# Another order of the steps, and 58 dummy matmuls at 12 of the maxima's and exponentials' steps

## The chip, the cores and the metric

The kernel runs on one core of a Trainium2 chip. The metric is the device time of one execution in microseconds (us), as the median of several runs. Five engines work side by side, each on its own list of instructions in program order: TensorE (PE, matmuls; its weight loads are shown apart as PEld), VectorE (DVE), ScalarE (ACT), GpSimd (POOL) and SyncE (SP, which issues most transfers). They wait for each other through semaphores alone.

## The reference, cut to what matters

The input x is 4 batches of 512 tokens of 128 features. The result is x plus two branches of its layer norm xn:

```
x  = L0_attn_x                       # (4, 512, 128)
xn = layernorm(x)
attn = Wo( chunk_attention(xn, chunk=16) + chunk_attention(every third token of xn, chunk=16) )
h  = xn + mla(rmsnorm(xn))           # 16 heads, causal attention over 512 tokens, latent q and k/v, rope
ffn = h + moe(rmsnorm(h))            # a shared expert and 7 routed ones, 2 picked for each token
out = x + attn + ffn
```

Everything is in float32. In `mla` the causal scores need the maximum of each row before the exponential, so the scores are computed twice: once with queries in the rows for the maxima, once transposed with the maxima already subtracted.

## The kernel before, in words

The work is cut into 760 steps. A table, ORDER (L152 on), names them in one sequence, and every engine walks through that same sequence and issues its own part of each step it has one in. So the table sets the order of work on every engine, and the semaphores alone set when it happens. A step is written as kind and numbers, the first number being the batch 0 to 3:

- LN, STATS, ROOT, XT, MA, MB, MV, WF: layer norm statistics, transposes of the normalised tokens, and the projections of the causal attention. ST are the transfers of the split bf16 parts of q and k into two stacks, SHIFT turns the maxima of one group of four heads into rows of the q stack.
- S (maxima): scores of one unit into a bank of ring A (two PSUM banks); VectorE reduces them to `neg_max` (L1012).
- E (exponentials): the same scores transposed into a bank of ring B (three banks), which ScalarE reads through the exponential into `p_mla` (L830). PV multiplies those with v into `bank_c`, Y, YT, X1 carry the result on.
- LQ, LK, LV, KD, VD, LS, LR, PT, LO, LT, LW: the two chunked attentions. LS also writes into ring A.
- R2, R3, X2T, ROUTE, PICK: second norm and routing. GU and DOWN: the eight experts, 32 steps of each; GU uses ring B, DOWN ring A.

A `*` in the table stands for the next maxima step and, once there is one, the next exponentials' step; `*3` for three of them. There are 176 maxima and 176 exponentials' steps, and the exponentials run 22 steps behind the maxima. Where an S stands directly ahead of an E, TensorE issues the two together, matmul by matmul (L1180 for E, L1159 for S, then the masks, L1166): one works on 64 rows of the array, the other on the other 64. TensorE waits for both banks (`wait_free`) before such a pair.

WARM (L64) is a table of dummy matmuls ahead of certain steps: float32, `eye` times `eye`, 128 columns, into `bank_c` (L1192). There are 30 of them.

Of the kernel before, what the change touches and what calls it, by code (L numbers as in the profile page):

```python
# [167 lines left out]
LR.2.2 *2 PT.2.2 PICK.0.0 LT.2.1 * LS.2.3 LO.2.2 PICK.0.1 LR.2.3 ST.3.2 * PICK.0.2 PV.2.0.1 PT.2.3 * LT.2.2 *
PV.2.0.2 PV.2.0.3 LS.2.4 MV.3 *3 KD.3.0 SHIFT.2.2 *3 PICK.0.3 * Y.2.0 R2.1 * ST.3.3 PV.2.1.0 KD.3.1 * KD.3.2 LO.2.3
KD.3.3 R3.1 ST.3.4 ST.3.5 LR.2.4 PV.2.1.1 * PV.2.1.2 PT.2.4 *3 X2T.1 * SHIFT.2.3 PV.2.1.3 * ST.3.6 * LT.2.3 *2 Y.2.1  # L170
PV.2.2.0 * LO.2.4 VD.3.0 * LS.3.0 LR.3.0 ROUTE.1 PV.2.2.1 PV.2.2.2 LT.2.4 *2 LW.2 PT.3.0 * PV.2.2.3 ST.3.7 SHIFT.3.0
* LS.3.1 * Y.2.2 PV.2.3.0 *2 LO.3.0 LR.3.1 * PT.3.1 *3 LT.3.0 LS.3.2 LO.3.1 PV.2.3.1 * PV.2.3.2 PV.2.3.3 VD.3.1
LR.3.2 *2 SHIFT.3.1 Y.2.3 PT.3.2 LT.3.1 PICK.1.0 PICK.1.1 LS.3.3 YT.2 LO.3.2 PICK.1.2 *2 LR.3.3 PICK.1.3 X1.2
PV.3.0.0 PT.3.3 *5 LT.3.2 * PV.3.0.1 * SHIFT.3.2 LS.3.4 PV.3.0.2 * PV.3.0.3 *3 Y.3.0 *2 WX LO.3.3 LR.3.4 * PV.3.1.0
* PT.3.4 * LT.3.3 PV.3.1.1 LO.3.4 * PV.3.1.2 PV.3.1.3 SHIFT.3.3 LT.3.4 *3 Y.3.1 * LW.3 R2.2 *3 PV.3.2.0 *4 PV.3.2.1
PV.3.2.2 *2 PV.3.2.3 *2 Y.3.2 *4 R3.2 PV.3.3.0 * PV.3.3.1 *2 GU.0.0 GU.0.1 PV.3.3.2 PV.3.3.3 DOWN.0.0 Y.3.3 GU.0.2
DOWN.0.1 GU.0.3 DOWN.0.2 GU.0.4 YT.3 DOWN.0.3 GU.0.5 DOWN.0.4 GU.0.6 DOWN.0.5 X1.3 GU.0.7 DOWN.0.6 R2.3 GU.1.0
DOWN.0.7 GU.1.1 R3.3 X2T.2 DOWN.1.0 GU.1.2 DOWN.1.1 GU.1.3 ROUTE.2 PICK.2.0 X2T.3 DOWN.1.2 GU.1.4 DOWN.1.3 PICK.2.1
GU.1.5 DOWN.1.4 GU.1.6 DOWN.1.5 PICK.2.2 GU.1.7 DOWN.1.6 PICK.2.3 ROUTE.3 GU.2.0 DOWN.1.7 GU.2.1 PICK.3.0 DOWN.2.0
GU.2.2 DOWN.2.1 GU.2.3 DOWN.2.2 GU.2.4 PICK.3.1 DOWN.2.3 GU.2.5 DOWN.2.4 GU.2.6 PICK.3.2 DOWN.2.5 GU.2.7 DOWN.2.6  # L180
GU.3.0 PICK.3.3 DOWN.2.7 GU.3.1 DOWN.3.0 GU.3.2 DOWN.3.1 GU.3.3 DOWN.3.2 GU.3.4 DOWN.3.3 GU.3.5 DOWN.3.4 GU.3.6
DOWN.3.5 GU.3.7 DOWN.3.6 DOWN.3.7
# [1232 lines left out]
```

How the kernel before makes its waits and increments, by code:

```python
        def wait_full(eng, use):  # L452
            ring, i, n = where[use]
            eng.wait_ge(full[ring][i], n)
# [1 line left out]
        def wait_drained(eng, use):  # L457
            ring, i, n = where[use]
            eng.wait_ge(drained[ring][i], n)
# [1 line left out]
        def wait_free(eng, use):  # L462
            ring, i, n = where[use]
            if n > 1:
                eng.wait_ge(drained[ring][i], n - 1)
# [21 lines left out]
        @block.sync  # L488
# [26 lines left out]
                kind, b = step[0], step[1] if len(step) > 1 else 0  # L515
                if kind == "LV" and step[2] == (QUADS - 1) // 4:
                    for n in range(step[2] + 1):
                        wait_drained(sp, ("LV", b, n))
                    for top in range(2):
                        n, at = P - CHUNK * (1 - top), P + CHUNK * (2 * top - 1)
                        sp.dma_start(v_dram[b, top, 0:n], v_rows[0:n, 0:X // 2]).then_inc(v_out, 16)
                        sp.dma_start(v_dram[b, top, at:at + P], v_rows[:, X // 2:]).then_inc(v_out, 16)
                if kind == "VD":
                    i0, i1 = SEGMENTS[step[2]]
                    sp.wait_ge(v_out, V_OUT * (b + 1))
                    if step[2]:
                        wait_full(sp, ("LO", b, LOCAL_UNITS - 1))
                    elif b:
                        wait_full(sp, ("LO", b - 1, NLU - 1))
                    else:
                        sp.wait_ge(v_zeroed, 1)
                    for top in range(2):
                        of = v_dram[b, top, CHUNK * top:CHUNK * top + 2 * P, :, i0:i1, :].rearrange(
```

## Time and profile before

| | us |
|---|---|
| median of 3 runs | 375.98 |
| lowest and highest | 373.47, 378.34 |
| the profiled execution | 371.83 |
| its span, first to last instruction | 369.6 |

In that execution TensorE is busy 90% of the span, VectorE 77%, ScalarE 60%, GpSimd 33%. The first maxima step stands at 26 us, the first exponentials' step at 60 us, the first expert at 273 us. In the rows further down a busy time is in us unless it says ns, "x8" counts instructions, "idle before" is how long the engine had nothing running just ahead, and the name behind the arrow is what released it.

### The profile page before, as it was taken

The numbers are of one execution on the slowest core, as the hardware profiler recorded it, in microseconds if no ns is written. First come the engines' busy times: TensorE is split into PE (matmuls) and PEld (weight loads), VectorE is DVE, ScalarE is ACT, GpSimd is POOL, SyncE is SP. The second block draws the span as 40 slices with busy tenths as digits, with TensorE's granted clock in tenths as the row PEclk, the third lists the DMA queues.
The fourth block names the chain that finished last, engine by engine and source line by source line (L and its number), as shares of the span: only waits on it lengthen the run. The fifth ranks groups of instructions, "written<-read, shape, count | busy, mean of one in ns | idle before, by whom it ended". The sixth has DMA issues, their size and how long they took to land.

```text
span 369.6 us, 11664 instructions
## 1 busy us (share of the span) xinstructions
PE 334.2 (90%) x4504; PEld 206.3 (56%) x4504; DVE 285.0 (77%) x720; ACT 222.3 (60%) x545; POOL 123.0 (33%) x148
## 2 busy tenths in 40 slices
...
PEclk9999999999999989999998999989999999999998
...
GB/s 200 77 108 173 71 167 62 67 62 42 40 162 46 36 66 51 78 184 25 43 53 50 65 65 34 36 3 172 5 0 0 3 27 2 4 28 2 29 0 28
DMA packets 29141, 21.84 MB, mean 59 GB/s; under 512 B 12312, under 2 KB 26008, under 8 KB 29048
## 3 DMA queue, kind: packets, MB, share of 16 engines
...
q10 hardware_dynamic: 216, 0.20, 0.2%
...
## 4 chain that ended last, share of the span: by engine, by line
PE 60%; DVE 28%; issue 5%; ACT 3%; DMA 3%; SPq 1%; POOL 0%; DVEq 0%; ACTq 0%; POOLq 0%
PE bank_B L1372 13%; DVE neg_max L1012 9%; PE bank_B L1180 8%; PE bank_c L1276 7%; PE bank_A L1378 7%; PE bank_A L1318 3%; PE bank_M L1283 2%; PE bank_B L1166 2%; DVE s_loc L1029 2%; DVE row_max L1026 2%; PE bank_M L1341 2%; PE bank_M L1221 2%; PE bank_c L1192 2%; PE bank_M L1211 1%; PE bank_M L1326 1%
## 5 line engine op out<-in xcount | busy, mean ns | idle before, releaser
L830 ACT ACTIVATE p_mla<-bank_B 128x512 f32<-128x512 f32 (+1 forms) x176 | 92.0, 561 | 54.6 <-PE bank_B L1166 31.0
L1012 DVE TENSOR_REDUCE neg_max<-bank_A 128x1 f32<-128x512 f32 (+3 forms) x176 | 106.9, 636 | 15.8 <-PE bank_A L1166 13.0
L1180 PE MATMUL bank_B<-q_stack,k_stack 54*128 54x512 bf16 (+3 forms) x256 | 62.4, 306 | 12.1 <-DVE neg_max L1012 8.2
L1159 PE MATMUL bank_A<-k_stack,q_stack 52*128 52x512 bf16 (+3 forms) x256 | 63.1, 307 | 3.2 <-DMA q_stack<-parts 2.2
L1372 PE MATMUL bank_B<-xrT,k_diag 128*128 128x512 f32 x128 | 60.9, 597 | 1.1 <-DVE k_diag L1137 1.1
L703 POOL TENSOR_TENSOR x<-x,q_part 128x512 f32<-128x512 f32 x31 | 39.5, 1274 | 58.0 <-ACT q_part L864 41.7
L1276 PE MATMUL bank_c<-p_mla,v_mla 128*32 128x384 f32 (+12 forms) x512 | 47.6, 453 | 0.4 <-ACT p_mla L830 0.4
L1180 PEld LDWEIGHTS bank_B<-q_stack,k_stack 54*128 54x128 bf16 x256 | 19.4, 94 | 49.6 <-issue 23.4
L864 ACT ACTIVATE q_part<-bank_A,expert_w 128x128 f32<-128x128 f32 x108 | 30.8, 369 | 24.6 <-PE bank_A L1378 24.6
L1137 DVE SCALAR_TENSOR_TENSOR k_diag<-k_diag,bank_B 128x512 f32<-128x512 f32 x32 | 22.0, 687 | 29.1 <-ACT k_diag L848 26.7
L1166 PE MATMUL bank_A<-masks 64*128 64x64 bf16 (+2 forms) x352 | 43.9, 204 | 0.0
L1166 PE MATMUL bank_B<-masks 64*128 64x64 bf16 (+2 forms) x352 | 43.8, 204 | 0.0
L1378 PEld LDWEIGHTS bank_A<-k_diag 128*128 128x128 f32 x256 | 33.1, 191 | 14.1 <-issue 14.1
L1166 PEld LDWEIGHTS bank_B<-masks 64*128 64x128 bf16 x352 | 32.6, 97 | 12.8 <-issue 0.9
L609 POOL TENSOR_TENSOR nrm<-nrm,half 128x8 f32<-128x8 f32 (+1 forms) x8 | 10.7, 1332 | 73.4 <-DVE nrm L1088 65.1
L1378 PE MATMUL bank_A<-k_diag 128*128 128x128 f32 x256 | 33.9, 275 | 0.7 <-DVEq L1145 0.7
L1166 PEld LDWEIGHTS bank_A<-masks 64*128 64x128 bf16 x352 | 32.8, 97 | 1.8
L1372 PEld LDWEIGHTS bank_B<-xrT,k_diag 128*128 128x128 f32 x128 | 21.6, 191 | 18.0 <-issue 13.6
L1142 DVE TENSOR_TENSOR k_diag<-bank_B,k_diag 128x512 f32<-128x512 f32 x32 | 22.1, 691 | 1.1
L1159 PEld LDWEIGHTS bank_A<-k_stack,q_stack 52*128 52x128 bf16 x256 | 19.3, 94 | 6.3 <-issue 3.7
L848 ACT ACTIVATE k_diag<-bank_B 128x512 f32<-128x512 f32 x32 | 19.5, 610 | 3.6 <-PE bank_B L1372 3.6
L1318 PE MATMUL bank_A<-k_diag,q_part 128*32 128x128 f32 x544 | 20.1, 277 | 0.7 <-DVE neg_max L1012 0.7
...
## 6 DMA issues: line engine op xcount, KB each, us to landing
...
```

The source lines that it names most:

```text
L703: link(nc.gpsimd.tensor_tensor(x[:, tb, :], x[:, tb, :], weighted[down_no[step] % 2], ALU.add))
L830: drained_by(nc.scalar.activation(p_of(n)[:, m:m + len(heads), 0:w], src, ACT.Exp, scale=SCALE), step)
L864: ins = nc.scalar.activation(weighted[n % 2][:, i, :], down[:, i, :], ACT.Copy, scale=expert_w[:, c * NT + i, e - 1:e])
L1012: drained_by(nc.vector.tensor_reduce(neg_max[:, g, m:m + len(heads), i], src, AX.X, ALU.max, negate=True), step)
L1142: ins = nc.vector.tensor_tensor(hid[n % 2], bank_of(step + (1,))[:], hid[n % 2], ALU.mult)
L1159: return nc.tensor.matmul(bank_of(step)[:, n * w:(n + 1) * w], q_stack[b % 2][rows, h % 8, i * P:(i + 1) * P], k_stack[b % 2][rows, h % 8, ...
L1166: return nc.tensor.matmul(to, half_eye[half, low, :], triangle[half, :].unsqueeze(1).broadcast_to((SLOT, len(heads), SLOT)), start=False, ...
L1180: nc.tensor.matmul(bank_of(step)[:, m * w:(m + 1) * w], k_stack[b % 2][rows, h % 8, j * P:(j + 1) * P], q_stack[b % 2][rows, h % 8, j * P: ...
L1276: last = nc.tensor.matmul(bank_c[32 * m:32 * m + width, j * P:], heads[:, first:first + width], p_of(n)[:, m, 0:S - j * P], start=(j == 0) ...
L1318: last = nc.tensor.matmul(bank[PAIR * j:PAIR * j + PAIR, c:c + P], q_part[:, a, pair, :], k_diag[:, a, :, CHUNK * pair:CHUNK * pair + CHUN ...
L1372: full_by(nc.tensor.matmul(bank_of(use)[:], w_exp[:, e, m, :], x2T[:, c, :], start=True, stop=True), use)
L1378: last = nc.tensor.matmul(bank[:, i * D:(i + 1) * D], hid[n % 2][:, i * P:(i + 1) * P], w_exp[:, e, 2, :], start=True, stop=True)
```

## The change

Three things change, and nothing else: each of the 760 steps is still there once, with the same work in it.

First, ORDER is another sequence. A third of the steps keep their place in it, over half move by one to three places, and the farthest moves by 27. Second, WARM is another table: 37 dummy float32 matmuls, all ahead of the matmuls of the first maxima step; the ten that stood one each ahead of the maxima steps 2 to 11 of batch 0 are gone. Third, FILLS adds 58 dummy bf16 matmuls of 128 rows and 192 columns at 12 steps: at three maxima steps of batch 0 into `bank_c`, at nine exponentials' steps into the very bank of ring B that the step then overwrites. At a pair they stand behind the wait for the bank of E and ahead of the wait for the bank of S.

```diff
-WARM = {("WF",): 6, ("XT", 0, 1): 2, ("MA", 0, 0): 2, ("S", 0, 0): 10, **{("S", 0, n): 1 for n in range(2, 12)}}
+WARM = {("LK", 0): 3, ("MA", 0, 0): 3, ("MA", 0, 1): 3, ("MB", 0): 1, ("MV", 0): 4, ("S", 0, 0): 16, ("WF",): 4, ("XT", 0, 0): 3}
+FILLS = {
+    1: """
+    E.1.0.2.0 E.3.1.0.2
+    """,
+    2: """
+    S.0.13
+    """,
+    3: """
+    S.0.16 S.0.21
+    """,
+    5: """
+    E.2.2.1.1
+    """,
+    6: """
+    E.2.1.1.2 E.2.1.2.1
+    """,
+    7: """
+    E.2.0.2.0
+    """,
+    8: """
+    E.0.0.1.2 E.2.0.1.2 E.3.0.0.3
+    """,
+}
+FILL = {(word[0], *(int(n) for n in word[2:].split("."))): count for count, words in FILLS.items() for word in words.split()}
+FILL_WIDTH = 192
...
-LN.0 WF XT.0.1 MA.0.0 MB.0 MA.0.1 XT.0.0 ST.0.0 LK.0 LQ.0 STATS.1 ST2.0 MV.0 ROOT LV.0.0 KD.0.0 * KD.0.1 * KD.0.2
+LN.0 WF XT.0.1 MA.0.0 MB.0 MA.0.1 XT.0.0 LK.0 LQ.0 STATS.1 ST.0.0 ST2.0 MV.0 LV.0.0 KD.0.0 KD.0.1 *2 LV.0.1 ROOT *
...
+            def fill(step, to):
+
+                for _ in range(FILL.get(step, 0)):
+                    nc.tensor.matmul(to[:, 0:FILL_WIDTH], masks[:, 0:P], masks[:, 0:FILL_WIDTH], start=True,
+                                     stop=True, skip_group_check=True)
...
-                if step in where and kind != "SHIFT":
-                    wait_free(pe, step)
+                if step in where:
                     bank = bank_of(step)
+                    if kind not in ("S", "E", "SHIFT"):
+                        wait_free(pe, step)
...
                     if step not in waits_for_e:
+                        fill(step, bank_c)
+                        wait_free(pe, step)
...
                     other = beside.get(step)
+                    if other:
+                        wait_free(pe, step)
+                        fill(step, bank)
+                        wait_free(pe, other)
+                    else:
+                        if step in FILL:
+                            wait_free(pe, next_down[step])
+                            fill(step, bank_of(next_down[step]))
+                        wait_free(pe, step)
```

Three places show what moves. The first is VectorE in batch 1, around the step that turns the maxima of the third group of heads into shift rows (`shift`). `s_loc` and `row_max` belong to the last LS of the batch, `y_loc` to an LO. Before:

```order
L1012 TENSOR_REDUCE neg_max<-bank_A 128x2 x2
L1012 TENSOR_REDUCE neg_max<-bank_A 128x4
L1026 TENSOR_REDUCE row_max<-bank_A 64x16
L1029 TENSOR_TENSOR s_loc<-bank_A,row_max 64x256
L1040 RECIPROCAL rden<-bank_M 128x32
L1043 TENSOR_TENSOR y_loc<-bank_M,rden 128x128 x2
L1019 CAST shift<-bank_M 16x128
L1020 TENSOR_TENSOR shift<-bank_M,shift 16x128
L1012 TENSOR_REDUCE neg_max<-bank_A 128x1 x6
```

And the same place with the change:

```order
L1041 TENSOR_REDUCE neg_max<-bank_A 128x2 x2
L1055 TENSOR_REDUCE row_max<-bank_A 64x16
L1058 TENSOR_TENSOR s_loc<-bank_A,row_max 64x256
L1041 TENSOR_REDUCE neg_max<-bank_A 128x4
L1069 RECIPROCAL rden<-bank_M 128x32
L1072 TENSOR_TENSOR y_loc<-bank_M,rden 128x128 x2
L1048 CAST shift<-bank_M 16x128
L1049 TENSOR_TENSOR shift<-bank_M,shift 16x128
L1041 TENSOR_REDUCE neg_max<-bank_A 128x1 x6
```

One reduction now stands between the LS and the LO; six other instructions stood in a row before, four do now.

The second is VectorE in batch 0, just ahead of the first exponentials. `rot` is the rope of q for batch 1. Before:

```order
L961 TENSOR_TENSOR rot<-bank_M,rope 128x512
L965 TENSOR_TENSOR rot<-rot,turned_q 64x512
L1012 TENSOR_REDUCE neg_max<-bank_A 128x4
L1026 TENSOR_REDUCE row_max<-bank_A 128x32
L1029 TENSOR_TENSOR s_loc<-bank_A,row_max 128x512
L1012 TENSOR_REDUCE neg_max<-bank_A 128x1 x4
```

With the change:

```order
L990 TENSOR_TENSOR rot<-bank_M,rope 128x512
L994 TENSOR_TENSOR rot<-rot,turned_q 64x512
L1055 TENSOR_REDUCE row_max<-bank_A 128x32
L1058 TENSOR_TENSOR s_loc<-bank_A,row_max 128x512
L1041 TENSOR_REDUCE neg_max<-bank_A 128x4
L1041 TENSOR_REDUCE neg_max<-bank_A 128x1 x4
```

Here the reduction that stood between the rope and the LS has moved behind both.

The third is TensorE in batch 2, at one of the two exponentials' steps with six dummies; the numbers behind the banks are which of the ring it is. With the change:

```order
L1201 MATMUL bank_B2<-masks 128x64
L1201 MATMUL bank_A1<-masks 128x64
L1187 MATMUL bank_B0<-masks 128x192 x6
L1215 MATMUL bank_B0<-q_stack0,k_stack0 128x384
```

The six stand between the masks of one pair and the first matmul of the next; before, nothing stood there.

## Rows read from the trace of the kernel before

**Rows 1.** The page: engines, granted clock in 40 slices, one group of weight loads

```profile
PE 334.2 (90%) x4504; PEld 206.3 (56%) x4504; DVE 285.0 (77%) x720; ACT 222.3 (60%) x545; POOL 123.0 (33%) x148
...
PEclk9999999999999989999998999989999999999998
...
L1166 PEld LDWEIGHTS bank_B<-masks 64*128 64x128 bf16 x352 | 32.6, 97 | 12.8 <-issue 0.9
```

**Rows 2.** The page, the chain that ended last, by engine

```profile
PE 60%; DVE 28%; issue 5%; ACT 3%; DMA 3%; SPq 1%; POOL 0%; DVEq 0%; ACTq 0%; POOLq 0%
```

**Rows 3.** Busy time by stretch: length, engines, then PEclk, DMA share, GB/s

```profile
26.00:62.00 36.00, 32.17 (x511) 21.14 (x511) 31.57 (x65) 18.92 (x44) 18.67 (x27) 1.00 0.42 120
62.00:275.00 213.00, 195.39 (x3454) 115.47 (x3451) 174.38 (x450) 140.08 (x339) 47.94 (x69) 0.97 0.26 61
275.00:364.00 89.00, 87.54 (x430) 55.55 (x428) 58.53 (x129) 51.29 (x148) 40.54 (x32) 1.00 0.03 10
```

**Rows 4.** Who waited for whom: us in total, times, longest

```profile
PE bank_B L1180 <- DVE neg_max L1012: 8.2, 19, 1.1
```

**Rows 5.** VectorE and TensorE around 130 us, in order of time

```profile
129.42 0.41 DVE L1026 TENSOR_REDUCE row_max<-bank_A 64x16 f32<-64x256 f32 x1
...
131.85 3.01 DVE L1012 TENSOR_REDUCE neg_max<-bank_A 128x1 f32<-128x512 f32 x5
...
132.58 0.39 PE L1180 MATMUL bank_B<-q_stack,k_stack 54*128 54x512 bf16 x1 [1.00 <-DVE neg_max L1012]
```

**Rows 6.** The same view around 60 us

```profile
59.52 0.69 DVE L1012 TENSOR_REDUCE neg_max<-bank_A 128x4 f32<-128x512 f32 x1
...
61.59 0.39 PE L1180 MATMUL bank_B<-q_stack,k_stack 54*128 54x512 bf16 x1 [0.87 <-DVE s_loc L1029]
```

**Rows 7.** 10 us stretches of the view of rows 3

```profile
60.00:70.00 10.00, 7.96 (x141) 4.21 (x141) 8.02 (x17) 5.90 (x14) 3.14 (x4) 0.83 0.30 84
...
240.00:250.00 10.00, 8.28 (x107) 3.94 (x105) 8.37 (x19) 6.35 (x17) 0.00 (x0) 0.83 0.01 3
```

**Rows 8.** 2 us stretches of the same view

```profile
70.00:72.00 2.00, 0.89 (x18) 0.53 (x18) 1.38 (x3) 1.44 (x5) 0.00 (x0) 1.00 0.06 11
...
132.00:134.00 2.00, 1.06 (x14) 0.54 (x16) 2.00 (x4) 1.92 (x5) 0.00 (x0) 1.00 0.30 43
...
136.00:138.00 2.00, 2.00 (x13) 1.63 (x16) 1.40 (x10) 0.90 (x2) 0.45 (x1) 0.51 0.33 96
```

**Rows 9.** The chain in order of time: a dummy, and MV of two batches

```profile
29.59 0.42 PE bank_c L1192 x2
...
134.97 2.00 PE bank_M L1227 x8
...
191.69 1.09 PE bank_M L1227 x8
```

**Rows 10.** Back-to-back bf16 matmuls of TensorE, in order of time

```profile
45.96 0.32 PE L1159 MATMUL bank_A<-k_stack,q_stack 52*128 52x384 bf16 x1
46.12 0.22 PE L1166 MATMUL bank_A<-masks 64*128 64x64 bf16 x2
```

**Rows 11.** Ten dummies of before in a row, in the same view

```profile
21.31 2.31 PEld L1192 LDWEIGHTS bank_c<-eye 128*128 128x128 f32 x20 [0.20 <-issue]
21.32 2.50 PE L1192 MATMUL bank_c<-eye 128*128 128x128 f32 x20
```

**Rows 12.** TensorE at two pairs in a row, same view

```profile
192.71 0.39 PE L1180 MATMUL bank_B<-q_stack,k_stack 54*128 54x512 bf16 x1
...
193.00 0.38 PE L1180 MATMUL bank_B<-q_stack,k_stack 54*128 54x512 bf16 x1
```

**Rows 13.** The first microseconds, in order of time

```profile
8.22 1.12 DVE L946 TENSOR_SCALAR xr<-x,mv,nrm 128x128 f32<-128x128 f32 x4
8.73 1.22 PE L1192 MATMUL bank_c<-eye 128*128 128x128 f32 x4
...
26.06 0.37 PE L1159 MATMUL bank_A<-k_stack,q_stack 52*128 52x512 bf16 x1 [2.24 <-DMA q_stack<-parts]
```

More of the change, by code:

```diff
@@ L168 @@
[L168 to L182, printed above, removed]
+LN.0 WF XT.0.1 MA.0.0 MB.0 MA.0.1 XT.0.0 LK.0 LQ.0 STATS.1 ST.0.0 ST2.0 MV.0 LV.0.0 KD.0.0 KD.0.1 *2 LV.0.1 ROOT *
@@ new lines @@
+KD.0.2 KD.0.3 *2 LN.1 *2 LV.0.2 XT.1.0 VD.0.0 STATS.2 LS.0.0 LR.0.0 * LK.1 LQ.1 *2 PT.0.0 * LS.0.1 * LV.1.0 *
+SHIFT.0.0 * LV.1.1 *2 LV.1.2 LO.0.0 *2 LR.0.1 PT.0.1 LT.0.0 LS.0.2 XT.1.1 LO.0.1 VD.0.1 * MA.1.0 MB.1 MV.1 *2 MA.1.1
+LR.0.2 PT.0.2 LT.0.1 LS.0.3 *5 ST.1.0 LO.0.2 LR.0.3 ST.1.1 * ST.1.2 PV.0.0.0 * SHIFT.0.1 * ST.1.3 ST.1.4 ST.1.5 *
+PT.0.3 *3 LT.0.2 LS.0.4 PV.0.0.1 ST.1.6 * PV.0.0.2 *2 PV.0.0.3 * SHIFT.0.2 LO.0.3 LR.0.4 *2 Y.0.0 PV.0.1.0 PT.0.4 *4
+LT.0.3 LO.0.4 KD.1.0 KD.1.1 * PV.0.1.1 KD.1.2 * SHIFT.0.3 LT.0.4 PV.0.1.2 PV.0.1.3 *4 Y.0.1 *2 PV.0.2.0 VD.1.0 *2
@@ new lines @@
+* PV.1.1.2 KD.2.3 PV.1.1.3 * ST.2.4 XT.3.0 * SHIFT.1.3 * LK.3 Y.1.1 *2 PV.1.2.0 R2.0 *2 LQ.3 ST.2.5 LV.3.0 *2 LV.3.1
+R3.0 ST.2.6 *2 PV.1.2.1 ST.2.7 PV.1.2.2 VD.2.0 * LV.3.2 XT.3.1 * SHIFT.2.0 LS.2.0 X2T.0 MA.3.0 ST.3.0 * PV.1.2.3
+LR.2.0 * ROUTE.0 * Y.1.2 *2 MB.3 * PV.1.3.0 PT.2.0 LS.2.1 * LO.2.0 PV.1.3.1 LR.2.1 * PT.2.1 * PV.1.3.2 * MA.3.1
+PV.1.3.3 * LT.2.0 Y.1.3 LS.2.2 ST.3.1 * YT.1 LO.2.1 X1.1 *2 VD.2.1 SHIFT.2.1 *2 LR.2.2 * PICK.0.0 PV.2.0.0 * PT.2.2
+LT.2.1 ST.3.2 PICK.0.1 LS.2.3 LO.2.2 LR.2.3 PICK.0.2 * PICK.0.3 * PV.2.0.1 PT.2.3 PV.2.0.2 LT.2.2 LS.2.4 * KD.3.0
@@ new lines @@
+MV.3 *2 SHIFT.2.2 PV.2.0.3 *4 LO.2.3 R2.1 Y.2.0 * ST.3.3 PV.2.1.0 KD.3.1 KD.3.2 KD.3.3 LR.2.4 ST.3.4 *2 R3.1 PT.2.4
+* PV.2.1.1 PV.2.1.2 ST.3.5 * SHIFT.2.3 * X2T.1 PV.2.1.3 ST.3.6 *3 VD.3.0 *3 Y.2.1 * LT.2.3 PV.2.2.0 LO.2.4 * LS.3.0
+PV.2.2.1 LR.3.0 ST.3.7 PV.2.2.2 ROUTE.1 LT.2.4 *2 LW.2 * PV.2.2.3 SHIFT.3.0 * PT.3.0 LS.3.1 * Y.2.2 PV.2.3.0 *2
+LO.3.0 LR.3.1 *2 PT.3.1 LT.3.0 LS.3.2 * LO.3.1 VD.3.1 PV.2.3.1 * PV.2.3.2 * PV.2.3.3 SHIFT.3.1 * LR.3.2 * Y.2.3
+PT.3.2 PICK.1.0 PICK.1.1 LT.3.1 LS.3.3 LO.3.2 PICK.1.2 YT.2 *2 X1.2 LR.3.3 PV.3.0.0 PICK.1.3 *2 PT.3.3 *3 LT.3.2 *
@@ new lines @@
+PV.3.0.1 * PV.3.0.2 SHIFT.3.2 LS.3.4 *2 WX LO.3.3 LR.3.4 PV.3.0.3 *2 Y.3.0 *2 PV.3.1.0 PT.3.4 *2 LT.3.3 LO.3.4 *2
+PV.3.1.1 PV.3.1.2 *3 PV.3.1.3 R2.2 LT.3.4 *2 SHIFT.3.3 LW.3 * Y.3.1 * PV.3.2.0 *4 PV.3.2.1 PV.3.2.2 *2 PV.3.2.3 *3
+Y.3.2 *3 PV.3.3.0 * PV.3.3.1 *2 GU.0.0 GU.0.1 DOWN.0.0 R3.2 PV.3.3.2 PV.3.3.3 GU.0.2 Y.3.3 DOWN.0.1 GU.0.3 DOWN.0.2
+GU.0.4 YT.3 DOWN.0.3 GU.0.5 DOWN.0.4 X1.3 R2.3 GU.0.6 X2T.2 DOWN.0.5 R3.3 GU.0.7 DOWN.0.6 GU.1.0 DOWN.0.7 GU.1.1
+ROUTE.2 PICK.2.0 X2T.3 DOWN.1.0 GU.1.2 DOWN.1.1 GU.1.3 DOWN.1.2 GU.1.4 DOWN.1.3 GU.1.5 DOWN.1.4 PICK.2.1 PICK.2.2
```

27 lines of the change are left out of this document (13 added, 14 removed).

## The prediction, made before the changed kernel ran

> **What bounds the kernel now.** I read the page first, then the chain, then busy time by stretch, then the waits of TensorE and the engines' rows at its longest ones. The page says TensorE: 334.2 of 369.6 us [rows 1], and the chain runs through it for 60% and through VectorE for 28% [rows 2]. By stretch [rows 3] that splits. In the experts (275 to 364 us) TensorE has 87.54 of 89 us busy, so at most 1.5 us can be won there by order. From 62 to 275 us it idles 213 - 195.4 = 17.6 us, with VectorE busy for 174.4. From 26 to 62 us VectorE, with 31.57 of 36 us, does almost as much as TensorE with 32.17.
>
> In the middle the two hand work to and fro. When its banks are free TensorE issues a pair of S and E every 193.00 - 192.71 = 0.29 us [rows 12], but VectorE needs 3.01 / 5 = 0.60 us to reduce one [rows 5] and ring A has two banks. So in a run of pairs TensorE has about 0.3 us to spare at each, and it stands still longer where VectorE has other work ahead of a reduction: 8.2 us in 19 waits of this kind, up to 1.1 us [rows 4]. The reader should see two such places: 1.00 us at 132.58, ended by a reduction that started at 131.85 behind the LS, LO and shift work [rows 5], and 0.87 us at 61.59, ended by `s_loc` [rows 6].
>
> The clock is the other loss. The page shows a 9 nearly everywhere, with three 8s ahead of the end [rows 1]; by 10 us stretches four in the middle (60, 130, 190 and 240 us) read 0.83 [rows 7]. A missing 0.17 of 10 us is 1.7 us of full-clock work each, 6.8 us together; inside one the grant is 0.51, the lower of its two levels (1.2 against 2.4 GHz) [rows 8]. TensorE was thin ahead of that fall, 1.06 of 2 us busy at 132. But it was thinner at 70 us, 0.89 of 2 us, and no fall followed [rows 8], so which thin place costs a fall is not to be read off one row. What a fall costs a step: the projection MV took 2.00 us inside one and 1.09 us outside [rows 9], so 0.9 of 1.1 us came through; where TensorE waits for VectorE anyway less does. I put a fall at 1.0 to 1.7 us.
>
> **The change, part by part.** The sum is made against the profiled execution's own 371.83 us, which is its span of 369.6 and 2.2 us around it.
>
> *Ten dummies removed* ahead of the maxima steps 2 to 11 of batch 0. One takes 0.42 us between two such steps [rows 9]. All ten on the path would be 4.2 us, none of it 0. VectorE carries this stretch [rows 3], so most ran while TensorE waited for a reduction anyway. I take -1.0. They also kept TensorE busy between 28 and 42 us; without them one or two falls could appear, 1.0 to 1.7 us each. Ends: -4.2 and +3.4.
>
> *The start.* Two dummies ahead of the first transpose go: they ran from 8.73 to 9.95, while the data they hid (`xr`) was there at 8.22 + 1.12 = 9.34 [rows 13]; up to -0.6. One more dummy stands ahead of the first projection (1.22 / 2 = 0.6 us at the clock of that moment), up to +0.6. The six more ahead of the first maxima step, 2.50 / 10 = 0.25 us each [rows 11], are 1.5 us within the 2.24 us in which TensorE waited for the stacks' transfer at 26.06 [rows 13]; if that cover were gone they would cost 1.5. The others of the new table stand where TensorE waits for a drained bank. Together 0, ends -0.6 and +1.5.
>
> *The 58 dummies.* No bf16 matmul of all 128 rows is in the trace. By columns the nearest is 384 columns in 46.12 - 45.96 = 0.16 us [rows 10], so 192 take 0.08. With its own weight load (97 ns for the masks' [rows 1]) not hidden at all it would be 0.18. The ten float32 dummies in a row took 2.50 us for 20 passes, with 2.31 us of weight loads in the same time [rows 11], so loads and passes overlap almost fully; I take 0.10, bound by the load. That is 5.8 us, ends 4.6 and 10.4. Of the 58, 48 stand at seven steps in fives to eights, 4.8 us. The room is 7 x 0.3 = 2.1 us plus whatever longer waits stand there, of which the waits of rows 4 are the measure. The rest delays the pair, and behind it the exponential and the next reduction. The ten in small groups fit. I take +1.0, ends 0 and +8.3 (10.4 - 2.1).
>
> The Trainium skill, page "TensorE: Matmul & The Clock Gate", Part 3 on packing small matmuls, says that a weight load overlaps matmuls in flight only when its row group differs. The new dummies use all rows one after another; by that rule each would pay its load, and the sum would end at the 10.4 us side. Rows 11 speak against it: 20 loads and 20 passes over all rows fit in hardly more than the passes.
>
> *Falls avoided.* Of the nine exponentials' steps with dummies five are in the middle of batch 2 and one is at the start of batch 3, which is where the program stands at 180 to 207 and at 237 us: five groups of five to eight around the fall at 190, and one ahead of that at 240. If they work, two falls go: 2.0 to 3.4 us. I take -2.0; ends -6.8 (all four) and 0.
>
> *The order.* At 132 us the LS moves ahead of one reduction, so VectorE no longer has LS, LO and shift in a row: the row of work before 131.85 began at 129.42, 2.43 us [rows 5], and without the LS it is some 0.8 us shorter. That should end most of the 1.00 us wait. At 60 us it goes the other way: the reduction of 0.69 us [rows 6] moves behind the LS, so TensorE's bank comes free later; the 0.87 us wait can grow by 0.7. The other 17 waits are reshuffled likewise. No instruction is added on SP, GpSimd or ScalarE; the first stacks' transfers move past steps in which SP issues nothing, and on GpSimd the square root for batch 1 moves behind two of the four copies of q, so the norm of batch 1 may start later, which is what the +1.5 of the start has to hold if its cover there does. In the experts PICK and the norm steps of the last batches shift by some places, worth at most the 1.5 us of idle time. I take -0.5, ends -4 (half of the 8.2 us of waits) and +3 (as many waits merged as at 60 us, four times 0.7).
>
> **Sum:** -1.0 + 0 + 1.0 - 2.0 - 0.5 = -2.5, so 371.83 - 2.5 = 369.3 us for an execution like the profiled one. The three runs lie 1.6, 4.15 and 6.5 us above that; part of this may be more falls than four, which the dummies would also mend, so for the median I add 3.0 and not 4.15: **372.3 us**. (With 4.15 it is 373.5.)
>
> **The ways it can go.** Two per cent, 7.5 us, is about what a measurement of this kernel can tell from no change. It is faster below 368.5 us and slower above 383.5.
>
> A, the forecast, 0.47: some falls go, dummies cost a little, order is nearly a draw. 370 to 375 us.
>
> B, the falls are the kernel's real loss, 0.27. All four go (4 x 1.1 = 4.4 after the part that VectorE hides), the dummies stay hidden, the order saves 3: 371.83 - 1.0 - 4.4 - 3.0 = 363.4, and with 3.0 it is 366.4 us. For it speaks that the runs spread over 5 us, as falls that come and go would make them. Against it, only seven of the steps have enough dummies to matter and none is near 130 us but for a single one.
>
> C, no change, 0.16: the falls move to other thin places (the 70 us row shows that thinness alone does not tell), and places like that at 60 us outweigh those like that at 132 us. 371.83 - 1.0 + 1.0 + 1.5 = 373.3, with 4.15 it is 377.5 us. That the change does not do what it says belongs here too: if VectorE sets the middle, dummies in TensorE's waits move nothing.
>
> D, slower, 0.10. The dummies are not hidden: the wait for the bank of E already takes up the room, and each pays its load. 10.4 us come onto the path, no fall is avoided, and the order gives nothing: 371.83 + 10.4 = 382.2, with 3.0 it is 385.2 us. It decides once more than about 8 of those 10.4 us are exposed. Against it are rows 11 and the spare 0.3 us a pair. By the Trainium skill's rule above the 10.4 us would be right, though not that they are exposed.
>
> The range is 365.5 to 379.0 us: A and C whole, most of B, without D and without the last of B. It reaches past C for the end at which the missing ten dummies bring a fall. Faster by over 2%: 0.29 (B, and a little of A). Slower by over 2%: 0.11 (D, and C with two falls more). Within: 0.60.
>
> **What the profile after would show.** The ten: nothing between the reductions at 28 to 42 us, granted clock still 1.00 there. The dummies: a mean spacing near 0.10 us in their groups, and waits for `neg_max` behind them shorter than before by as much; if they are exposed, the chain holds them with several us. The falls: fewer than four stretches at 0.83. The order: a wait at the place of 132.58 below 0.5 us, one at the place of 61.59 of 1.2 us or more, and the total of 8.2 us down by one or two. The forecast is wrong if the clock shows as many falls and the time is down all the same (then the order was worth more than I gave it), or if the falls are gone and the time is not.

## The result, and the profile after

The changed kernel takes 376.12 us as the median of 20 runs (373.69 to 380.31); the kernel before took 373.40 beside it (20 runs, 369.76 to 385.05). The ratio is 1.0098, its 95% interval 1.0074 to 1.0122: it is 1% slower. Ratios, here and below, compare only those executions that are not over 1.5% above the fastest of their kernel, so a ratio can differ from that of the two medians. The forecast was 372.3 us and a gain.

The profiled execution took 376.22 us, 374.4 of it span, against 371.83 and 369.6. Its page, engines, granted clock in 40 slices and the chain's shares [rows 1, 2]:

```profile
PE 339.2 (91%) x4576; PEld 211.6 (57%) x4576; DVE 289.1 (77%) x720; ACT 222.6 (59%) x545; POOL 123.3 (33%) x148
...
PEclk9998999899999999999999999999999999999998
...
PE 62%; DVE 20%; issue 5%; ACT 5%; DMA 3%; POOL 2%; SPq 1%; DVEq 0%; ACTq 0%; POOLq 0%
```

TensorE has 5.0 us more of busy time, which is about what 58 dummies are (58 x 0.083 = 4.8 us). The clock has one 8 near 30 us and one near 70, and none where three stood between 130 and 250 us. Busy time by stretch, columns as in [rows 3, 7] (length, then PE, PEld, DVE, ACT, POOL, clock, DMA share, GB/s):

```profile
26.00:62.00 36.00, 30.64 (x493) 19.62 (x491) 30.72 (x64) 18.74 (x44) 18.47 (x26) 0.95 0.40 117
62.00:275.00 213.00, 195.52 (x3487) 117.39 (x3487) 175.18 (x446) 139.38 (x336) 49.18 (x70) 0.99 0.26 62
275.00:365.00 90.00, 87.93 (x441) 54.89 (x438) 59.88 (x132) 50.99 (x144) 38.49 (x31) 1.00 0.03 10
```

```profile
30.00:40.00 10.00, 8.19 (x72) 4.93 (x71) 9.09 (x27) 5.88 (x12) 7.28 (x9) 0.83 0.55 173
60.00:70.00 10.00, 8.44 (x167) 4.84 (x158) 7.91 (x16) 4.82 (x11) 3.81 (x5) 0.83 0.23 64
130.00:140.00 10.00, 8.27 (x181) 4.97 (x178) 8.96 (x21) 7.04 (x18) 5.10 (x8) 1.00 0.28 60
190.00:200.00 10.00, 8.60 (x178) 5.53 (x176) 8.72 (x34) 7.03 (x21) 0.96 (x2) 1.00 0.13 29
240.00:250.00 10.00, 8.92 (x188) 6.20 (x180) 9.15 (x34) 7.05 (x20) 0.00 (x0) 1.00 0.01 2
```

The clock of the middle is better (0.99 against 0.97) and the kernel is slower all the same. That is the case which the prediction named as the one in which it is wrong: fewer falls (two stretches at 0.83 in place of four) and the time not down. The waits of TensorE, as in [rows 4]:

```profile
PE bank_B L1215 <- DVE neg_max L1041: 8.1, 20, 0.9
...
PE bank_B L1419 <- DVE k_diag L1166: 2.1, 3, 1.1
PE bank_A L1365 <- issue: 1.6, 1, 1.6
...
PE bank_M L1388 <- DMA v_diag<-v_dram: 1.3, 1, 1.3
```

The wait for `neg_max` is as large as before, 8.1 against 8.2 us, and under it stand waits that were not there or were smaller. Others are gone, as that of 2.24 us at the first maxima step [rows 13]: in all TensorE idles 374.4 - 339.2 = 35.2 us, against 369.6 - 334.2 = 35.4 before. The largest of the new ones is ahead of the first LS of batch 1. SP's queue and what stood behind it, in order of time:

```profile
91.00 4.45 SPq L566 DMA_DIRECT2D v_diag<-v_dram  x8
95.49 3.00 SPq L597 DMA_DIRECT2D k_diag<-k_part  x4
...
100.34 0.43 PE L1365 MATMUL bank_A<-k_diag,q_part 128*32 128x128 f32 x8 [1.63 <-issue]
100.41 0.40 POOL L688 COPY k_part<-kT 64x256 f32<-64x256 f32 x1 [2.94 <-DMA k_diag<-k_part]
```

And the same part of SP's queue in the kernel before:

```profile
86.37 6.40 SPq L568 DMA_DIRECT2D k_diag<-k_part  x8
92.88 3.69 SPq L537 DMA_DIRECT2D v_diag<-v_dram  x8
```

Before, the last transfers of `k_diag` went out ahead of eight of `v_diag`; now the eight are ahead, and LS, which needs `k_diag`, stands still until the last four have landed: 1.63 us. In the table of steps that is VD.1.0 in front of KD.1.3.

**How the kernels are compared below.** Every run lists the span and the mean granted clock, and span times (1 - clock) is the clock it lost, in us. Over 92 runs of the kernel before, beside the experiments, the lost clock was 11.7 us on average (standard deviation 4.2), and a straight line through them is span = 364.0 + 0.83 x lost clock, with a correlation of 0.92. The runs of one kernel differ mostly by that. So each kernel has two figures here: its **full-clock span**, the mean of span - 0.9 x lost clock, with its standard error (0.9 was the slope in the first comparison, and is used throughout), and its mean lost clock. Both are taken over all its executions. For the kernel before they are 363.2 ± 0.16 and 11.7; for the changed kernel 369.4 ± 0.25 and 5.9. At full clock the change costs 6.2 us, and it gives part of that back in clock. With 0.83 in place of 0.9 it would be 5.8 us: a difference between a kernel that loses much clock and one that loses little carries up to 0.5 us of doubt from the slope. The mean lost clock of a kernel has a standard error of 0.4 to 1.5 us (over 2 in two kernels with six runs), so differences of 1 us in it say little. Differences at full clock are against this 363.2 in all that follows, unless another kernel is named.

### The profile page after: what moved, and what is told of

Read it like the earlier page. It is cut to its first block, busy times and chain, and to the rows that moved or that the text cites. A ratio compares the mean times of both kernels' runs of the same rounds, so it can differ in the third digit from the quotient of the medians.

```text
span 374.4 us, 11799 instructions
## 1 busy us (share of the span) xinstructions
PE 339.2 (91%) x4576; PEld 211.6 (57%) x4576; DVE 289.1 (77%) x720; ACT 222.6 (59%) x545; POOL 123.3 (33%) x148
## 4 chain that ended last, share of the span: by engine, by line
PE 62%; DVE 20%; issue 5%; ACT 5%; DMA 3%; POOL 2%; SPq 1%; DVEq 0%; ACTq 0%; POOLq 0%
PE bank_B L1419 11%; PE bank_B L1215 10%; PE bank_c L1323 8%; PE bank_A L1425 6%; DVE neg_max L1041 5%; PE bank_A L1365 3%; PE bank_M L1388 3%; PE bank_B L1201 2%; PE bank_M L1257 2%; ACT k_diag L803 2%; PE bank_M L1330 2%; PE bank_M L1373 2%; PE bank_M L1247 2%; PE bank_M L1252 1%; DMA v_dram<-v_rows 1%
## 5 line engine op out<-in xcount | busy, mean ns | idle before, releaser
L1041 DVE TENSOR_REDUCE neg_max<-bank_A 128x1 f32<-128x512 f32 (+3 forms) x176 | 107.2, 636 | 14.3 <-PE bank_A L1201 10.6
L1215 PE MATMUL bank_B<-q_stack,k_stack 54*128 54x512 bf16 (+3 forms) x256 | 61.6, 301 | 10.9 <-DVE neg_max L1041 8.1
L1323 PE MATMUL bank_c<-p_mla,v_mla 128*32 128x128 f32 (+11 forms) x512 | 46.1, 444 | 0.2 <-ACT p_mla L859 0.2
L638 POOL TENSOR_TENSOR nrm<-nrm,half 128x8 f32<-128x8 f32 (+1 forms) x8 | 10.7, 1343 | 68.0 <-DVE nrm L1117 60.3
```

The lines of the kernel that those rows point to most:

```text
L1041: drained_by(nc.vector.tensor_reduce(neg_max[:, g, m:m + len(heads), i], src, AX.X, ALU.max, negate=True), step)
L1215: nc.tensor.matmul(bank_of(step)[:, m * w:(m + 1) * w], k_stack[b % 2][rows, h % 8, j * P:(j + 1) * P], q_stack[b % 2][rows, h % 8, j * P: ...
L1323: last = nc.tensor.matmul(bank_c[32 * m:32 * m + width, j * P:], heads[:, first:first + width], p_of(n)[:, m, 0:S - j * P], start=(j == 0) ...
```

## The experiments

Four comparisons, each beside runs of the kernel before, which gave 376.64, 374.95, 373.93 and 377.37 us as medians, full-clock spans of 363.3, 363.5, 363.1 and 362.5 (± 0.2 to 0.4), and a lost clock of 11.9, 11.1, 10.7 and 15.2 us.

### First comparison: the parts of the change

**The new WARM alone.**

```diff
-WARM = {("WF",): 6, ("XT", 0, 1): 2, ("MA", 0, 0): 2, ("S", 0, 0): 10, **{("S", 0, n): 1 for n in range(2, 12)}}
+WARM = {("LK", 0): 3, ("MA", 0, 0): 3, ("MA", 0, 1): 3, ("MB", 0): 1, ("MV", 0): 4, ("S", 0, 0): 16, ("WF",): 4, ("XT", 0, 0): 3}
```

> The sequence of before, no bf16 dummies, the new table of 37 float32 dummies alone. Theory T (the new sequence costs, by transfers queued behind others on SP; the tables of dummies cost little): ratio to before 1.000 to 1.003. Rival W (the new float32 table costs: TensorE's clock rises later, 13.1 against 11.7 us, and falls at 33.5 us once the ten dummies of batch 0 are gone): the first exponentials 1.5 to 2.5 us later than before, ratio 1.004 to 1.008. Rival D (the 58 bf16 dummies cost): 1.000.

Measured: 372.94 us, ratio 1.0039 (0.9998 to 1.0079), full-clock span 363.4 ± 0.37, lost clock 8.8. The start and the ten removed dummies are worth nothing in sum (0.2 ± 0.4 us).

**The new ORDER alone.**

```diff
-LN.0 WF XT.0.1 MA.0.0 MB.0 MA.0.1 XT.0.0 ST.0.0 LK.0 LQ.0 STATS.1 ST2.0 MV.0 ROOT LV.0.0 KD.0.0 * KD.0.1 * KD.0.2
+LN.0 WF XT.0.1 MA.0.0 MB.0 MA.0.1 XT.0.0 LK.0 LQ.0 STATS.1 ST.0.0 ST2.0 MV.0 LV.0.0 KD.0.0 KD.0.1 *2 LV.0.1 ROOT *
...
```

> The new sequence alone, with the 30 float32 dummies of before and no bf16 dummies. T: LS of batch 1 still waits some 1.6 us for the transfers of k_diag at 100 us, the experts still have three waits for VectorE (2.1 us), ratio 1.007 to 1.012. W: ratio 0.998 to 1.004, since most of the loss is the start. D: 1.000 or below.

Measured: 377.18 us, ratio 1.0053 (0.9976 to 1.0129), full-clock span 366.9 ± 0.38, lost clock 8.6. One of the twelve executions took 759.79 us, at a granted clock of 1.00; nothing on record explains it, and it is in the median and not in the other figures. The order costs 3.7 us at full clock. The interval of the ratio cannot see it, because these runs lost 3 us less clock than those of before.

**The dummies alone**: the changed kernel's code with ORDER and WARM of before.

```diff
+FILLS = {
...
+}
...
+                    if other:
+                        wait_free(pe, step)
+                        fill(step, bank)
+                        wait_free(pe, other)
```

> The sequence and the float32 dummies of before, with the 58 bf16 dummies added at the same steps, and the waits for the two banks in the new order. T and W: the dummies are hidden and avoid a fall or two, ratio 0.994 to 1.000. D: they are exposed in part and raise the time, ratio 1.005 to 1.010.

Measured: 374.22 us, ratio 1.0087 (1.0046 to 1.0128), full-clock span 367.9 ± 0.37, lost clock 7.2. So 4.7 us for dummies and turned waits together; the dummies take TensorE 6.04 us in the trace from the first dummy of each group to the step behind it, summed over the twelve groups.

**The changed kernel without its dummies.**

```diff
+FILL = {}
```

> The changed kernel without its 58 bf16 dummies: new sequence, new float32 dummies. T and W: as the changed kernel or slower, since clock falls come back, ratio to before 1.009 to 1.015 against 1.010 with them. D: ratio 1.000 to 1.004.

Measured: 378.63 us, ratio 1.0194 (1.0111 to 1.0276), full-clock span 369.8 ± 0.74, lost clock 7.3. The dummies are gone, the loss is not: against the changed kernel's 369.4 their removal is worth -0.4 ± 0.8 us. It is also 2.9 ± 0.8 us above the new order alone (366.9), from which it differs by WARM, worth nothing, and by the code around the dummies; the fourth comparison comes back to this.

### Second comparison: where the order loses

**VD.1.0 ahead of KD.1.3, and nothing else.** It turns two groups of transfers in SP's queue.

```diff
-PV.0.2.0 KD.1.3 * * LN.2 PV.0.2.1 * VD.1.0 * LW.0
+PV.0.2.0 VD.1.0 KD.1.3 * * LN.2 PV.0.2.1 * * LW.0
```

> The kernel before with one step moved: the 8 transfers of VD (v_diag) of batch 1 go ahead of the last 4 transfers of k_diag on SP's queue, as in the changed kernel; every other engine has its list of before. To be read apart: the span, and what of it is lost clock (span times one minus the mean granted clock); over the 29 runs of before in the first comparison the span was 363.2 us plus 0.9 of the lost clock. Theory Q (the new sequence loses first of all by this queue): LS of batch 1 waits 1.2 to 1.7 us near 98 us, the full-clock span rises by 1.2 to 2.0 us. Rival S (the loss is spread over many small swaps): the wait is absorbed behind VectorE, the full-clock span rises by less than 0.5.

Measured: 374.19 us, ratio 1.0010 (0.9963 to 1.0058), full-clock span 365.7 ± 0.45, lost clock 7.2. SP's queue, and TensorE behind it:

```profile
88.63 4.75 SPq L537 DMA_DIRECT2D v_diag<-v_dram  x8
93.42 2.90 SPq L568 DMA_DIRECT2D k_diag<-k_part  x4
```

```profile
98.14 0.43 PE L1318 MATMUL bank_A<-k_diag,q_part 128*32 128x128 f32 x8 [2.17 <-issue]
```

The trace shows a new wait of 2.17 us, and the full-clock span is 2.5 ± 0.5 us longer. Both are above what was expected (1.7 and 2.0 at most).

**The new order of the experts alone**: behind the second DOWN of batch 0 the new sequence; the first step that differs is the 693rd of 760.

```diff
-GU.0.5 DOWN.0.4 GU.0.6 DOWN.0.5 X1.3 GU.0.7 DOWN.0.6 R2.3 GU.1.0 DOWN.0.7 GU.1.1 R3.3 X2T.2
+GU.0.5 DOWN.0.4 X1.3 R2.3 GU.0.6 X2T.2 DOWN.0.5 R3.3 GU.0.7 DOWN.0.6 GU.1.0 DOWN.0.7 GU.1.1
...
```

> The kernel before up to the second DOWN of batch 0, then the changed kernel's sequence of the experts, with its other places of the norm, routing and PICK steps. Q: three waits of TensorE for VectorE in the experts (2.1 us in the changed kernel) in place of one of 0.8, full-clock span +1.0 to +1.5. S: below +0.5.

Measured: 378.81 us in six runs, which give no ratio and no interval; full-clock span 364.5 ± 0.25, lost clock 14.3. One of its waits:

```profile
PE bank_B L1372 <- DVE k_diag L1137: 2.1, 3, 1.1
```

In the kernel before that row reads 1.1 us in 2 waits, the longest 0.8. The 1.0 us more fits the 1.3 ± 0.3 us of the full-clock span.

**The rest of the order**: the new sequence with these two places put back (VD.1.0 behind KD.1.3, experts as before), in the code of before, WARM of before, no dummies. Against the new sequence:

```diff
-PV.0.2.0 VD.1.0 * * PV.0.2.1 LN.2 KD.1.3 * * LW.0
+PV.0.2.0 * * PV.0.2.1 LN.2 KD.1.3 * VD.1.0 * LW.0
```

> The new sequence without these two: VD of batch 1 back behind the k_diag transfers, and the experts as before; float32 dummies of before, no bf16 dummies. The new sequence whole had a full-clock span 3.6 us above before. Q: +0 to +1.2 is left. S: +2.5 or more is left.

Measured: 370.83 us, ratio 0.9895 (0.9840 to 0.9949), full-clock span 363.7 ± 0.32, lost clock 5.4. At full clock the rest of the order is nearly a draw (+0.5 ± 0.4 us), and this kernel is 1% faster because it loses half as much clock. It has no new dummy.

**Twice the dummies**, on the kernel with the dummies alone.

```diff
+FILL = {step: 2 * n for step, n in FILL.items()}
```

> Sequence and float32 dummies of before, with twice the bf16 dummies at the same 12 steps (116). Theory X (a group of dummies ends after the bank it was to cover, so each further dummy is exposed in full): full-clock span +4.5 to +5.5 us above the kernel with 58, which was 4.6 above before. Rival H (half of them are hidden behind VectorE's reductions): +2 to +3. The lost clock stays at 6 to 7 us, as with 58, if it is set by other places; it falls further if dummies are what holds the clock.

Measured: 380.81 us, ratio 1.0171 (1.0069 to 1.0272), full-clock span 374.1 ± 0.72, lost clock 8.1. The second 58 cost 6.2 ± 0.8 us, more than was expected, and brought no clock that six runs could show (8.1 ± 2.1 against 7.2 ± 1.0).

### Third comparison: the changed kernel mended

**The two places put back in the changed kernel**, WARM and dummies kept.

```diff
-PV.0.2.0 VD.1.0 * * PV.0.2.1 LN.2 KD.1.3 * * LW.0
+PV.0.2.0 * * PV.0.2.1 LN.2 KD.1.3 * VD.1.0 * LW.0
...
```

> The changed kernel with all its dummies, but VD of batch 1 back behind the k_diag transfers and the experts in the sequence of before. Theory Q+X (those two places and the exposed dummies are the loss): full-clock span 2.5 to 3.5 us below the changed kernel's 369.4, so 366 to 367, still 3 above before's 363.4 because of the dummies; lost clock 5 to 7 us; time within 0.3% of before. Rival (the two places no longer matter once dummies stand in the way): above 368.

Measured: 371.85 us, ratio 0.9974 (0.9940 to 1.0007), full-clock span 366.7 ± 0.43, lost clock 3.8. The span came as expected, the lost clock is below the 5 to 7 us expected.

**The same with at most three dummies at a step** (31 instead of 58), WARM of before.

```diff
+FILL = {step: min(n, 3) for step, n in FILL.items()}
```

> The sequence without the two bad places, float32 dummies of before, and the bf16 dummies cut to at most 3 a step (31 instead of 58). X with room (each step has 0.3 us to spare, and a group costs 0.08 a dummy plus 0.10 at its end): groups of 3 last 0.35 us, so 0 to 0.1 us is exposed at each, full-clock span 364 to 365 against 363.7 without. Rival (any dummy ahead of a pair is exposed from the first on): 366 or more.

Measured: 372.01 us, ratio 0.9952 (0.9910 to 0.9993), full-clock span 366.6 ± 0.35, lost clock 4.7. Half of the dummies gone and not 0.2 us saved (0.1 ± 0.6), 1.6 us above what was expected at most, and as the rival had it: something in the code costs time whatever the number of dummies.

**The mended sequence without dummies, with the new WARM**, in the code of before.

```diff
-WARM = {("WF",): 6, ("XT", 0, 1): 2, ("MA", 0, 0): 2, ("S", 0, 0): 10, **{("S", 0, n): 1 for n in range(2, 12)}}
+WARM = {("LK", 0): 3, ("MA", 0, 0): 3, ("MA", 0, 1): 3, ("MB", 0): 1, ("MV", 0): 4, ("S", 0, 0): 16, ("WF",): 4, ("XT", 0, 0): 3}
```

> The sequence without the two bad places, no bf16 dummies, and the new table of 37 float32 dummies in place of the 30 of before. If the float32 table costs nothing, as the first comparison had it (363.4 against 363.3): full-clock span 363.4 to 364.2. If it costs with this sequence (TensorE then waits 1.3 us for v_diag at 47 us, as in the changed kernel's profile): 365 or more.

Measured: 369.84 us, ratio 0.9878 (0.9834 to 0.9922), full-clock span 363.5 ± 0.51, lost clock 5.3. By its ratio it is the fastest kernel of this study, 1.2% below the one before; the same sequence with the old WARM (0.9895) can't be told from it.

### Fourth comparison: the order of two waits

In the kernel before, TensorE waits ahead of a pair of S and E first for the bank of S, which the reduction to `neg_max` frees and which mostly ends last, and then for the bank of E, directly ahead of the matmuls. The change turned the two, at every one of the 154 pairs (176 less the 22 by which the exponentials run behind) and not only where dummies stand. The traces of the runs so far show what follows, from the end of the reduction that frees the bank to the first matmul of the pair. At the pairs that start within 0.2 us of that end, with TensorE idle just before (31 in the kernel before, 31 in the changed one), the median is 56 to 58 ns in every kernel with the old order of waits, and 146 or 147 ns in every kernel with the new one.

**The kernel before with only the two waits turned.**

```diff
-                    wait_free(pe, step)
+                    if step not in waits_for_e:
+                        wait_free(pe, step)
...
                     other = beside.get(step)
+                    if other:
+                        wait_free(pe, other)
```

> The kernel before, with one thing changed: at a pair the wait for the bank of S now stands behind the wait for the bank of E, as in the changed kernel, in place of ahead of it. No dummies, no other order. Theory V (the wait that ends last must not be the last one ahead of the matmul: 146 in place of 57 ns at each pair that VectorE holds up): full-clock span +2 to +3 us over before, the latency in the trace 140 to 150 ns. Rival X (the loss is the dummies' own time): +0 to +0.5 and 57 ns.

Measured: 377.14 us, ratio 1.0113 (1.0025 to 1.0201), full-clock span 366.3 ± 0.33, lost clock 10.1. Turning them costs 3.1 ± 0.4 us at full clock (3.8 ± 0.5 against the kernel before in this comparison alone), with no compute instruction added and no step moved; 35 pairs in its trace are held up in that way, and 35 x 0.09 = 3.2. One of them, VectorE and then TensorE:

```profile
192.33 0.69 DVE L1012 TENSOR_REDUCE neg_max<-bank_A 128x4 f32<-128x512 f32 x1
```

```profile
193.14 0.09 PEld L1180 LDWEIGHTS bank_B<-q_stack,k_stack 54*128 54x128 bf16 x1 [0.49 <-issue]
...
193.17 0.37 PE L1180 MATMUL bank_B<-q_stack,k_stack 54*128 54x512 bf16 x1 [0.28 <-DVE neg_max L1012]
193.17 0.09 PEld L1159 LDWEIGHTS bank_A<-k_stack,q_stack 52*128 52x128 bf16 x1
```

The reduction ends at 193.02 and the first matmul starts 0.15 us later, with its weight load 0.03 us ahead. In the kernel before it reads so:

```profile
132.57 0.09 PEld L1180 LDWEIGHTS bank_B<-q_stack,k_stack 54*128 54x128 bf16 x1 [1.27 <-DVE neg_max L1012]
```

That load and the matmul of 132.58 [rows 5] lie within 0.01 us. A second sign is who is named ahead of the load at the pairs:

```profile
PEld bank_B L1180 <- issue: 23.4, 54, 1.2
...
PEld bank_B L1180 <- DVE neg_max L1012: 20.0, 44, 1.3
```

so in the kernel before; with the waits turned, and in the changed kernel,

```profile
PEld bank_B L1180 <- issue: 46.0, 100, 2.1
```

```profile
PEld bank_B L1215 <- issue: 42.1, 100, 1.2
```

That the late wait stands last is not enough for the 90 ns. In the kernels with the turned order two kinds of pair still start 56 to 58 ns after the reduction, with the load 4 ns ahead. One kind is the second and the third pair of a kernel: they use their bank of ring B for the first time, `wait_free` issues no wait for that, and so the wait for the bank of S is the only one. The fourth pair has both, and shows 146 to 148 ns. In the changed kernel the second pair:

```profile
63.17 0.09 PEld L1215 LDWEIGHTS bank_B<-q_stack,k_stack 54*128 54x128 bf16 x1 [0.41 <-DVE neg_max L1041]
63.17 0.39 PE L1215 MATMUL bank_B<-q_stack,k_stack 54*128 54x512 bf16 x1 [0.30 <-DVE neg_max L1041]
```

The other kind has dummies between its two waits that end before the reduction does. In the kernel with at most three dummies at a step there are four such places, one of them this:

```profile
185.90 0.09 PEld L1216 LDWEIGHTS bank_B<-q_stack,k_stack 54*128 54x128 bf16 x1 [0.50 <-DVE neg_max L1042]
185.91 0.33 PE L1216 MATMUL bank_B<-q_stack,k_stack 54*128 54x384 bf16 x1 [0.28 <-DVE neg_max L1042]
```

There are 17 such pairs in seven traces. So in these traces the 90 ns go with a late wait that directly follows another wait, with no matmul between them.

**The dummies alone, with the waits turned only at the steps that have dummies.**

```diff
+                        if step not in FILL:
+                            wait_free(pe, other)
                         wait_free(pe, step)
-                        fill(step, bank)
-                        wait_free(pe, other)
+                        if step in FILL:
+                            fill(step, bank)
+                            wait_free(pe, other)
```

> Sequence and float32 dummies of before with the 58 bf16 dummies, but the two waits turned only at the nine exponentials' steps that have dummies. With all waits turned it was 4.6 us above before. V: +1.5 to +2.5 is left, the exposed part of the dummies. X: still +4 to +5.

Measured: 378.55 us, ratio 1.0115 (1.0016 to 1.0213), full-clock span 366.8 ± 0.67, lost clock 9.9. Of the 4.7 us of the dummies' kernel 1.1 ± 0.8 belong to the waits; the dummies themselves, with the waits at their own steps, cost 3.6 ± 0.7 here, which lies between the two expectations. Against the kernel with the waits alone turned (366.3) the dummies cost 1.6 ± 0.5.

**The mended kernel with the same edit.**

> The changed kernel with all its dummies, the two bad places of the sequence mended, and the waits turned only at steps with dummies. V: full-clock span 1.5 to 3 us below the 366.7 of its twin, so about 364.5, time 0.8 to 1.2% below before. X: 366 to 367.

Measured: 370.38 us, ratio 0.9921 (0.9844 to 0.9999), full-clock span 365.0 ± 0.42, lost clock 3.9. That is 1.7 ± 0.6 below its twin.

**The same with at most three dummies at a step.**

> As e14 with at most 3 bf16 dummies a step (31). V: 363.5 to 364.5, and if these few dummies still hold the clock (4 to 5 us lost in place of 11), the fastest of all: 1.2 to 1.6% below before. X: 366 to 367.

Measured: 369.97 us, ratio 0.9929 (0.9847 to 1.0012), full-clock span 365.3 ± 0.51, lost clock 3.9. Fewer dummies gained nothing here either, against the expectation, within 0.7 us of error. The traces show why there was little to gain. With all dummies, four of the seven large groups end at most 0.07 us past the point at which the pair could start (57 ns behind the reduction), a fifth 0.12, and only two lie open in full; with three a step four groups are hidden and three lie open, 0.34 to 0.35 us each. That makes 1.6 against 1.0 us in the open.

## Why the prediction was wrong

Taken apart from the changed kernel downwards, at full clock:

| step | full-clock span | difference |
|---|---|---|
| the changed kernel | 369.4 | |
| two places of the order put back | 366.7 | -2.7 ± 0.5 |
| waits turned back where no dummies stand | 365.0 | -1.7 ± 0.6 |
| dummies and their waits gone | 363.5 | -1.5 ± 0.7 |
| the kernel before | 363.2 | -0.3 ± 0.5 |

That is 6.2 us. Against it stands the clock. The changed kernel loses 5.9 us of it. For the kernel before beside it an estimate has to do, since its clocks in those runs are not on record: its median of 373.40, with 2.0 us around the span as in the 92 runs, is a span of 371.4, 8.2 above 363.2, or 9.1 us of clock lost at 0.9. The difference of 3.2, times 0.9, is 2.9 given back: 6.2 - 2.9 = 3.3, against the measured 376.12 - 373.40 = 2.7. Each part alone on the kernel before costs as much as its line here or more (order 3.7 ± 0.4, waits 3.1 ± 0.4, dummies 1.6 ± 0.5 or 3.6 ± 0.7); that they share the same slack is my reading of it, not shown.

The 376.12 us lie inside the forecast range, and that is luck: of the two parts that cost most one stood in the sum as a gain and the other not at all, and the clock took back about half. The reference was off as well. The 3.0 us added for the median came from three runs; over twenty the median of the kernel before is only 1.6 above its profiled execution, so the sum's -2.5 stood for 370.9 us.

*The order, forecast -0.5, measured +2.7 ± 0.5 (two places taken out of the change) to +3.7 ± 0.4 (put alone into the kernel before).* This is the step that failed most. I looked at VectorE at two places and took waits of TensorE for VectorE as all there is to win or lose. The sentence "no instruction is added on SP" is true and beside the point: two groups already in its queue changed places, and the one that TensorE waits for went last. The wait for it is 1.63 us in the changed kernel, and 2.17 us with a loss of 2.5 us when nothing else is changed. About 1 us more is lost in the experts, where I looked only for a gain ("at most the 1.5 us of idle time") and not for new waits. The end of +3 is about what came, though for another reason.

*The two waits, no term in the sum, measured +1.7 ± 0.6 to +3.1 ± 0.4.* The section on the change says that three things change, "and nothing else". The waits are a fourth: its diff shows them, its words tell of them only at steps with dummies, and the prediction passes over them. That the edit touches every pair could be seen without a run; that it costs 90 ns at each that waits is told by no row of before.

*The 58 dummies, forecast +1.0, measured from -0.4 ± 0.8 (in the changed kernel) over +1.5 ± 0.7 (in the mended one) to +3.6 ± 0.7.* Their price was right, 0.10 us each: in the changed kernel

```profile
201.65 0.67 PE L1187 MATMUL bank_B<-masks 128*128 128x192 bf16 x6
202.25 0.33 PE L1215 MATMUL bank_B<-q_stack,k_stack 54*128 54x384 bf16 x1
```

six and the change back to half rows take 0.60 us, no wait after them. What was mis-sized is the room. I gave each group 0.3 us "plus whatever longer waits stand there". At five of the seven large groups the changed kernel's trace bears that out: the pair starts 0.06 to 0.20 us after the end of the reduction, so the dummies fill a wait and run over it by 0.14 us at most. At the other two (205.80 and 242.06 us) the bank had been free for over 2 us, and six and eight dummies lie open, 0.60 and 0.76 us. The sentence of the Trainium skill (page "TensorE: Matmul & The Clock Gate", Part 3) that a weight load overlaps matmuls in flight only when its row group differs would have made them 10.4 us; six in 0.60 us speak against it, as rows 11 did.

*The ten dummies, forecast -1.0, and the start, 0: together 0.* The kernel with the new WARM alone has the full-clock span of before, 363.4 against 363.3. Only the sum is measured; that the ten lay where TensorE waited anyway is likely and not shown. The clock from 28 to 42 us was to stay at 1.00; in this execution it is 0.83 in the ten us from 30 on, as shown above. The new WARM alone still lost less clock on average (8.8 against 11.9), and the kernel with only the waits turned, which has the ten, reads 0.59 from 30 to 40 us, so this one fall says little.

*Falls avoided, forecast -2.0, in effect about -2.9 by the estimate above.* Right in sign; its cause is not shown. I reckoned from one execution with four stretches at 0.83, 6.8 us [rows 7]; the kernel before loses 11.7 us on average. The profiled execution was one of its better ones, so the +3.0 to the median was clock as well and not a constant of the measurement. The dummies alone do lower the lost clock of the kernel before, from 11.9 to 7.2 us, but so does nearly every other change to it: the new WARM gives 8.8, turning two groups in SP's queue 7.2 (from 11.1), turning the waits 10.1 (from 15.2). With no dummy the mended sequence loses 5.3 or 5.4. The lost clock follows the sequence in a way that I cannot read from it. The mended kernels with all dummies or half of them lose 3.8 to 4.7, at most 1.4 ± 0.9 us under that without, and pay 1.5 us for it.

*The signs.* Fewer than four stretches at 0.83: yes, two. Dummy spacing near 0.10: 0.083. The total for `neg_max` down by one or two: no, 8.1. The place of 132.58 below 0.5 us: no, its like in the changed kernel waits 0.87 us. The place of 61.59 at 1.2 or more: no, 0.80. Both readings in order of time:

```profile
62.42 0.37 PE L1215 MATMUL bank_B<-q_stack,k_stack 54*128 54x512 bf16 x1 [0.80 <-DVE s_loc L1058]
...
137.44 0.37 PE L1215 MATMUL bank_B<-q_stack,k_stack 54*128 54x512 bf16 x1 [0.87 <-DVE neg_max L1041]
```

The rows of VectorE that moved there did not set these waits in the way I worked out: an LS less ahead of the reduction shortened the one by 0.13 us (0.09 of the 0.87 are the turned waits), an LS more did not lengthen the other.

*The rivals.* D, all dummies exposed at 10.4 us and no fall avoided, is refuted in its price; that they are exposed in part is true. C came nearest in time (377.5 us), but its reasons were falls that move and waits like that at 60 us, and neither is what was found. B is half right: lost clock costs the kernel before some 10 us (11.7 x 0.9), yet the mended sequence recovers over half of that without any new dummies.

**Left open.** Why a late wait that directly follows another wait is answered 90 ns later; shown is where it is, and that the weight load then stands 31 ns ahead of the matmul instead of 4. What in a sequence makes the clock fall. Whether the parts share their slack, as their prices alone and together suggest.
